# Expert slots of 128 tokens, projection stores from two queues, third parts on VectorE, and a later reciprocal, in a 16-layer kernel

## What is computed

```python
score = einsum('bhqd,bhkd->bhqk', q, k) / sqrt(HEAD_DIM)
attn = softmax(where(causal, score, -inf), axis=-1)
return einsum('bhqk,bhkd->bhqd', attn, v).transpose(0, 2, 1, 3).reshape(B, S, DIM) @ wo + bo
```

```python
expert_ids = argmax(softmax(einsum('btd,ed->bte', x, router_w)), axis=-1)
h = square(relu(einsum('btd,edh->ebth', x, expert_fc)))      # 128 -> 512 channels
out_e = einsum('ebth,edh->ebtd', h, expert_proj)             # 512 -> 128 channels
output = einsum('ebtd,bte->btd', out_e, one_hot(expert_ids))
```

## Time and profile before

| what | value |
|---|---|
| median of three runs | 6275.22 us |
| the profiled execution's own time | 6273.15 us |
| span of that execution on the engines | 6271.4 us |
| mean granted TensorE clock | 0.912 of full |
| TensorE busy | 4874.7 us (78%) |
| VectorE / ScalarE / POOL busy | 3773.5 / 3169.5 / 1644.0 us |

### The profile page before, as it was taken

How to read it: one execution, slowest core, us unless ns; L and a number is a source line. 1 busy time by engine, 2 the same in 40 slices (tenths; PEclk the granted TensorE clock), 3 DMA queues, 4 the chain that set the end, 5 groups by cost and what they waited for, 6 DMA issues and landing times. The chain is left out here.

```text
span 6271.4 us, 90519 instructions
## 1 busy us (share of the span) xinstructions
PE 4874.7 (78%) x33371; PEld 2083.9 (33%) x33466; DVE 3773.5 (60%) x4700; ACT 3169.5 (51%) x5938; POOL 1644.0 (26%) x1264
## 2 busy tenths in 40 slices
PE   5777658886678866688765887849976799688799
PEld 2232223332222235222253222326532244222244
DVE  6899546764677732778424876277738710578510
ACT  5665336665456732367512776534456521477621
POOL 0666137672211124311153111000005500311100
PEclk8999869998889988899986999969988999799999
DMA  0000031110312123321133111000000000101100
GB/s 25 0 1 0 4 101 31 38 36 18 95 34 46 36 62 98 107 45 40 41 99 119 34 41 42 8 10 2 2 13 0 19 0 1 59 23 40 40 0 14
DMA packets 150368, 222.90 MB, mean 36 GB/s; under 512 B 44966, under 2 KB 74514, under 8 KB 148564
## 3 DMA queue, kind: packets, MB, share of 16 engines
q1 hardware_dynamic: 144084, 209.16, 12.2%
q0 software_dynamic: 5888, 8.43, 0.4%
HBM read 137.92 MB, written 81.23 MB: 35 GB/s over the span
## 5 line engine op out<-in xcount | busy, mean ns | idle before, releaser
L914 ACT ACTIVATE l_core_probs<-l_core_ps_scores_b 128x512 f32<-128x512 f32 (+3 forms) x3840 | 1612.7, 500 | 983.7 <-PE l_core_ps_scores_b L826 780.1
L985 DVE TENSOR_REDUCE l_core_chunk_max<-l_core_ps_scores_a 128x2 f32<-128x1024 f32 (+3 forms) x1280 | 1272.1, 1022 | 344.4 <-PE l_core_ps_scores_a L807 180.2
L826 PE MATMUL l_core_ps_scores_b<-l_q_rows_sb,l_k_rows_sb 64*128 64x512 bf16 (+3 forms) x3840 | 943.5, 338 | 265.0 <-ACT l_core_probs L914 222.4
L807 PE MATMUL l_core_ps_scores_a<-l_k_rows_sb,l_q_rows_sb 64*128 64x512 bf16 (+3 forms) x3840 | 763.0, 346 | 252.4 <-DVE l_core_chunk_max L985 148.2
L942 POOL TENSOR_SCALAR_AFFINE_SELECT l_core_probs<-l_core_probs 128x512 f32<-128x512 f32 x512 | 327.3, 639 | 1804.8 <-ACT l_core_probs L914 1804.8
L826 PEld LDWEIGHTS l_core_ps_scores_b<-l_q_rows_sb,l_k_rows_sb 64*128 64x128 bf16 x3840 | 274.4, 94 | 1167.0 <-ACT l_core_probs L914 955.3
L845 PE MATMUL l_core_ps_acc<-l_core_probs,l_v 128*9 128x512 f32 (+3 forms) x6144 | 659.5, 502 | 0.0
L985 DVE TENSOR_REDUCE l_core_neg_max<-l_core_ps_scores_a 128x2 f32<-128x256 f32 (+3 forms) x640 | 504.5, 821 | 82.6 <-PE l_core_ps_scores_a L768 80.8
L1858 POOL TENSOR_TENSOR l_scan_bx<-l_xs,l_scan_b_rows 128x1024 f32<-128x1024 f32 x192 | 452.5, 2357 | 224.1 <-DVE l_scan_states L1868 217.8
L1868 DVE TENSOR_TENSOR_SCAN l_scan_states<-l_scan_ps_decay,l_scan_bx 128x1024 f32<-128x1024 f32 x192 | 439.8, 2290 | 40.7 <-POOL l_scan_bx L1858 15.3
L933 POOL TENSOR_TENSOR l_core_probs_decayed<-l_core_probs,l_decay 128x1536 f32<-128x1536 f32 (+2 forms) x160 | 392.0, 2476 | 218.0 <-ACT l_core_probs L914 217.9
(11 more groups left out here) (316 smaller groups left out, 7391.2 us busy)
## 6 DMA issues: line engine op xcount, KB each, us to landing
l_q_rows<-l_proj_parts SPq DMA_DIRECT2D x96, 256.0 KB, 5.7
l_k_rows<-l_proj_parts SPq DMA_DIRECT2D x96, 256.0 KB, 5.1
l_q_rows_sb<-l_q_rows SPq DMA_DIRECT2D x128, 192.0 KB
l_k_rows_sb<-l_k_rows SPq DMA_DIRECT2D x128, 192.0 KB
l_slots_weights<-m_both_dram SPq DMA_DIRECT2D x46, 512.0 KB
l_heads_out<-l_core_out_sums SPq DMA_DIRECT2D x300, 32.0 KB
l_q_rows_sb<-l_core_max_parts SPq DMA_DIRECT2D x480, 4.0 KB, 1.8
l_core_heads<-l_heads_out SPq DMA_DIRECT2D x15, 512.0 KB, 5.5
```

What stands on the lines that cost most here:

```text
L807: mm = nc.tensor.matmul(slot[:, i, 0:w], qs[n % 3][rows, p, qt * P:(qt + 1) * P], ks[n % 3][rows, p, c * NT:c * NT + w], start=True, stop= ...
L826: mm = nc.tensor.matmul(pb[(m + i) % 3][:, 0:w], ks[n % 3][rows, p, kt * P:(kt + 1) * P], qs[n % 3][rows, p, q0:q0 + w], start=True, stop= ...
L914: nc.scalar.activation(pt[:, ts % RP, j, 0:w], pb[m % 3][:, 0:w], ACT.Exp, scale=scale).then_inc(b_free, 1)
L985: nc.vector.tensor_reduce(to, pa[e % 2][:, :, 0:width_a(qt, c)], AX.X, ALU.max, negate=True).then_inc(a_free, 1)
```

## The change

It makes five edits.

1. Slots have 128 tokens instead of 256, so there are 39 instead of 23. Per slot there is one gather, one scatter, one transpose, four up products of 128 columns and four down products of 128 columns. Buffers: 8 for gathered rows, 8 for weights, 4 for result rows, two PSUM banks for the transpose and four for up. POOL runs gather(j), scatter(j - 6); TensorE's round j is transpose(j + 1), up(j), down(j - 2). The tables of `experts_route` follow.
2. Projection without rope (layers 2, 8, 14): the low part is made by VectorE, which does value(n) and then third(n - 3). Value n waits for the low part of n - 4. POOL keeps the remainder only. The loops over n are unrolled.
3. All projections: the six k stores of each sequence are issued by ScalarE's queue instead of SP's, after the second step of the next sequence, and for the last one at the end.
4. `max_rows` issues three DMAs, each for two partitions 64 apart, instead of six.
5. `invert(B - 1, 12)` moves from ahead of the first late unit to after the addition of late unit 3, ahead of scale_heads(5).

With rope POOL and VectorE do what they did.

```diff
@@ attn_project, sync
-                    for j, n in enumerate("qk"):
-                        for slot in range(6):
-                            sp.dma_start(parts[n]..., part[0:R, j, PAIRS[slot][j], b * S:(b + 1) * S]
+                    for slot in range(6):
+                        sp.dma_start(parts["q"]..., part[0:R, 0, PAIRS[slot][0], b * S:(b + 1) * S]
@@ attn_project, vector (no rope)
+                def plain_value(n):
+                    dve.wait_ge(mm_ready, n + 1)
+                    if n >= 4:
+                        dve.wait_ge(low, n - 3)
...
+                    dve.wait_ge(val, n + 1)
+                    dve.sem_inc(mm_free, 1)
+                def plain_third(n):
+                    dve.wait_ge(mid, n + 1)
+                    nc.vector.tensor_tensor(part[0:R, j, 2, tok], t1[0:R, j, h, :], part[0:R, j, 1, tok],
+                                            ALU.subtract).then_inc(low, 1)
+                    for n in range(4 * B):
+                        plain_value(n)
+                        if n >= 3:
+                            plain_third(n - 3)
+                    for n in range(4 * B - 3, 4 * B):
+                        plain_third(n)
@@ attn_project, scalar
+                def store_k(b):
+                    act.wait_ge(low, 4 * b + 4)
+                    for slot in range(6):
+                        act.dma_start(parts["k"]..., part[0:R, 1, PAIRS[slot][1], b * S:(b + 1) * S]
+                for b in range(B):
                     for m in range(4):
                         first(b, m)
                         if m:
                             second(b, m - 1)
+                        if b and m == 1:
+                            store_k(b - 1)
                     second(b, 3)
+                store_k(B - 1)
@@ attn_project, gpsimd: third, the wait for low and t_free only with rope
@@ attn_core
-        MIN = 16 * 6
+        MIN = 16 * 3
-                    for i in range(2):
-                        for e in range(3):
-                            row = 64 * i + r0 + e
-                            sp.dma_start(qs[u][row:row + 1, :, :].rearrange("o p (k q) -> o (p k) q", q=P),
-                                         mpart[16 * i:16 * i + 16, e, :]).then_inc(m_in, 16)
+                    for e in range(3):
+                        sp.dma_start(qs[u][r0 + e:r0 + e + 65:64, :, :].rearrange("i p (k q) -> i (p k) q", q=P),
+                                     mpart[:, e, :]).then_inc(m_in, 16)
@@ attn_core, vector, late
+                    if t == 3:
+                        invert(B - 1, 12)
                     if t + 2 < TILES:
                         scale_heads(t + 2)
...
                         scale_heads(1)
-                        invert(B - 1, 12)
@@ experts_slots
-SLOT = 2 * P
+SLOT = P
-    XR, YR, WR = 4, 3, 3
-    AHEAD = 3
+    XR, YR, WR = 8, 4, 8
+    AHEAD = 6
-        px = ps("turned_x", [P, NT])
-        pu = ps("up", [P, 2, HC, SLOT])
+        px = [ps(f"turned_x{n}", [P, NT]) for n in range(2)]
+        pu = ps("up", [P, 4, HC, SLOT])
...
-                    if j >= 2:
-                        pe.wait_ge(relu_done, j - 1)
+                    if j >= 4:
+                        pe.wait_ge(relu_done, j - 3)
                     for k in range(HC):
-                        mm = nc.tensor.matmul(pu[:, j % 2, k, :], ...
+                        mm = nc.tensor.matmul(pu[:, j % 4, k, :], ...
...
-                for j in range(SLOTS + 1):
+                for j in range(SLOTS + 2):
                     if j + 1 < SLOTS:
                         turn_in(j + 1)
                     if j < SLOTS:
                         up(j)
-                    if j >= 1:
-                        down(j - 1)
+                    if j >= 2:
+                        down(j - 2)
```

More of the change, by code:

```diff
@@ L501, in _ @@
                     sp.wait_ge(low, 4 * (b + 1))
[L502 to L506 removed]
+                    for slot in range(6):
+                        sp.dma_start(parts["q"].rearrange("(b h s d) t -> b s h d t", b=B, s=6, d=dq)[b, slot],
+                                     part[0:R, 0, PAIRS[slot][0], b * S:(b + 1) * S]
+                                     ).then_inc(stored if b else first_stored, 16)
                     if b == 0:
@@ L584, in second @@
                                          ACT.Copy).then_inc(mid, 1)
-                with act.Fori(0, B) as b:
+                def store_k(b):
+                    act.wait_ge(low, 4 * b + 4)
+                    for slot in range(6):
+                        act.dma_start(parts["k"].rearrange("(b h s d) t -> b s h d t", b=B, s=6, d=dq)[b, slot],
+                                      part[0:R, 1, PAIRS[slot][1], b * S:(b + 1) * S]
+                                      ).then_inc(stored if b else first_stored, 16)
+                for b in range(B):
                     for m in range(4):
@@ L614, in _ @@
                         remain(b, m)
-                        if m:
+                        if m and rope:
                             third(b, m - 1)
@@ L618, in _ @@
                             pool.sem_inc(t_free, 1)
-                    third(b, 3)
-                    pool.wait_ge(low, 4 * b + 4)
-                    pool.sem_inc(t_free, 1)
+                    if rope:
+                        third(b, 3)
+                        pool.wait_ge(low, 4 * b + 4)
+                        pool.sem_inc(t_free, 1)
 def attn_core(net, tag, w, dq, r0, scale, alibi, decay, out_bias, v, qs, ks, heads_out, sums, rsums, consts, c_in,
@@ L1067, in experts_route @@
         count = sb("count", [P, E, 1])
-        above = sb("above", [P, E, NTOK // 2])
+        above = sb("above", [P, E, NTOK])
         need = sb("slots_needed", [P, E + 1])
@@ L1309, in turn_in @@
                 def turn_in(j):
-                    pe.wait_ge(gathered[j % XR], 32 * (j // XR + 1))
-                    if j:
-                        pe.wait_ge(xt_ready, j)
-                    for i in range(2):
-                        mm = nc.tensor.transpose(px[:, i * P:(i + 1) * P], xg[:, j % XR, i, :], net.ident[:, :])
-                    mm.then_inc(px_ready, 1)
+                    pe.wait_ge(gathered[j % XR], 16 * (j // XR + 1))
+                    if j >= 2:
+                        pe.wait_ge(xt_ready, j - 1)
+                    nc.tensor.transpose(px[j % 2][:, 0:P], xg[:, j % XR, :], net.ident[:, :]).then_inc(px_ready, 1)
                 def up(j):
@@ L1330, in down @@
                         pe.wait_ge(yr_ready, j - 1)
-                    for i in range(2):
-                        for k in range(HC):
-                            mm = nc.tensor.matmul(py[j % 2][:, i * P:(i + 1) * P], h[:, j % 2, k, i * P:(i + 1) * P],
-                                                  wt[:, j % WR, (HC + k) * P:(HC + k + 1) * P],
-                                                  start=(k == 0), stop=(k == HC - 1))
+                    for k in range(HC):
+                        mm = nc.tensor.matmul(py[j % 2][:, 0:P], h[:, j % 2, k, :], wt[:, j % WR, (HC + k) * P:(HC + k + 1) * P],
+                                              start=(k == 0), stop=(k == HC - 1))
                     mm.then_inc(py_ready, 1)
                 turn_in(0)
-                for j in range(SLOTS + 1):
+                for j in range(SLOTS + 2):
                     if j + 1 < SLOTS:
@@ L1366, in y_rows @@
                     if j >= YR:
-                        act.wait_ge(scattered[j % YR], 32 * (j // YR))
-                    nc.scalar.copy(yr[:, j % YR, :, :], py[j % 2][:, 0:SLOT].rearrange("p (i c) -> p i c", i=2)).then_inc(yr_ready, 1)
-                for j in range(SLOTS + 1):
+                        act.wait_ge(scattered[j % YR], 16 * (j // YR))
+                    nc.scalar.copy(yr[:, j % YR, :], py[j % 2][:, 0:P]).then_inc(yr_ready, 1)
+                for j in range(SLOTS + 2):
                     if j < SLOTS:
                         relu(j)
-                    if j >= 1:
-                        y_rows(j - 1)
+                    if j >= 2:
+                        y_rows(j - 2)
             @block.vector
```

108 lines of the change are left out of this document (53 added, 55 removed).

## The result

The changed kernel took 6134.93 us in the median of four runs (6124.79 to 6136.52); the kernel before, on the same chip, 6276.62 (four runs, 6273.28 to 6287.34). The ratio is 0.9768, with a 95% interval from 0.9751 to 0.9785. The profiled execution took 6124.79 us, 148.4 less than that of before.

What follows compares the result with a forecast made beforehand. In the expert slots no engine was full: POOL waited for results and TensorE for gathers. From 6273.15 us, slots -105, reciprocal -31, maxima -19 and projection -9 gave 6109, stated as 6110; range 6080 to 6185.

Steps and rivals of the forecast that it cites:

- Slots, -105: Both expert stages: 111.7 us from first gather to last scatter instead of 164.0 and 164.7; -105 us for both.
- I take its waits in the middle at nothing: Expert slots: POOL, six slots ahead, waits nothing mid-stretch as long as other engines need under 2.71 us per slot.
- Rival E: Expert slots: gathers starve behind weight loads; at a landing of 12.5 us, +94 for the slots, 6308 in all; 3%.
- The reciprocal, -31: Last group of the attention cores: moving the reciprocal saves 6.2 us per layer, five layers; -31 us.
- The maxima, -19: Attention cores: three issues instead of six save 1.9 us at the first and last groups, five layers; -19 us.
- I leave it as it was: Landing of the maxima's DMAs, 1.8 us in the median and 3.2 at most, taken as unchanged.
- Projection, -9: Projections: -2 each in layers 2 and 8, 0 in layers 4 and 6, -5 in layer 14; -9 us.
- Four buffers of t1 take up most of that: Projections: buffers mostly absorb VectorE's and POOL's waits of up to 3.8 us behind ScalarE's six issues, three times per layer.
- +10 (every stall on the path): Upper end for all five projection layers together: +10 us, if every stall lies on the path.
- B: Expert slots: VectorE's squares obstruct POOL's DMAs, 3.4 us per slot; -57 instead of -105, 6158 us; 20%.
- C: Attention cores: the reciprocal's wait only moves, to the return of the inverse; 6141 us; 12%.
- D: Expert slots: TensorE stays at 1.2 GHz, 4.3 us per slot; +8 instead of -105, 6223 us; 4%.

Runs made afterwards that it cites:

- the first and the third group: Follow-up runs, each group of four kernels on one chip; the changed kernel without edit took 6166.23 us in the first and 6159.96 in the third.
- the run on record: The changed kernel's original profiled execution, against the kernel before: 6124.79 us.
- the second group: Four follow-up kernels on one chip: changed with six maxima DMAs 6156.87 us, slots' part alone 6170.91, changed with old ring and lead 6575.24, 256-token slots 6211.54.

## Why the prediction was right, and where not

The forecast was 6110 us, the result 6134.93; on the profiled executions -163 against -148.4.

**Slots, -105.** Right in size and in its steps: 112.7 and 109.9 us where 111.7 had been worked out, the first scatter 14.6 and 13.7 us after the first gather (13.5), a slot every 2.75 and 2.71 us on average while gathers and scatters alternate (2.71), most of them 2.65. By itself the part gave -102.5. On the chips of the first and the third group it gave less: the slots stages are 70 and 75 us shorter than in the profile of the kernel before, by late signals that nothing in the forecast stood for. The 6166 and 6160 us there lie in the range by its width, and not because their cause was foreseen. What the forecast took for granted was the lead: "I take its waits in the middle at nothing" holds at six and would have been wrong by 200 us per layer at three, which I had not worked out. Rival E has the chain spread over three slots; by the kernel's order it is four at a lead of six (gather j + 3 is issued right after scatter j - 4). Two small sums are off as well: the end at 1.30 us is -113, not -114, and E's slots come to +93, not +94.

**The reciprocal, -31.** Measured 35.7 over the cores and 33.4 on the clock. What was named as late next came as named: VectorE waits 3.31 us for the inverse (some 4 were forecast) and nobody behind it waits.

**The maxima, -19.** Measured 17.9 over the cores, 17.4 from the timelines before and after. "I leave it as it was", of the landing, held: 1.21 us after the end of the issues against 1.20. What was off is the 1.9 us at the first group, taken from layer 4 alone. In the other four layers the kernel before waits only 1.0 us there, so only that wait and some 0.2 us around it could be gained: the first groups gave 6.9 us in all where 9.5 had been taken, the last ones 10.5 where 9.5 had. That the sum came as near -19 as it did is in part luck. The Trainium skill (DMA: Bandwidth & Descriptors, "Why a DMA increments its semaphore by 16 and not by 1") has the merged DMA on two engines instead of sixteen, with the issuing sequencer writing the rest of the sixteen in one step. The trace agrees: the semaphore has 3 records for each merged DMA (144 for 48 in each layer) and 16 for each of one partition. The longer landing that the prediction took from this, and with it -16, is not there.

**Projection, -9.** Here the sign failed: +14.5. Layer 14 (-3.7, forecast -5; the sign named for it, at least 4 us, is just missed), layers 2 (-1.2) and 8 (+1.5) are within 4 us of the forecast. Layers 4 and 6 came out at +8.0 and +9.8. The step that failed is "Four buffers of t1 take up most of that", with its "0 in layers 4 and 6". Two things were wrong in it. The price of six issues was taken from SP alone, 0.63 us each, 3.8 in all; with SP's stores under way as well it was 7.22 and 6.74 us, and 3.79 only once. And with rotary positions VectorE, POOL and ScalarE pass each buffer round in a ring with no slack: of 7.2 us POOL waited 5.4 and TensorE 4.6. The upper end, "+10 (every stall on the path)", was 4.5 us too low for the same reason.

**The rivals.** B, POOL obstructed by VectorE, has not come, though the forecast's 0.4 us was seen. In the changed kernel's two stretches 49 indirect DMAs that overlapped a square alone took 1.03 us in the mean and 43 that overlapped a square and the copy 1.12, against 1.02 for the 36 that met nothing; in the kernel before, 42 that met a square took 1.19. That is some 5 us over both layers; 19 of the 92 that met a square took over 1.1 us, before 20 of 42. The Trainium skill (SBUF — State Buffer, "Who interferes with whom") says of a VectorE instruction like the square, a tensor_tensor with both inputs in SBUF, that it contends with POOL's reads, and infers that it leaves the writing of descriptors alone. The trace agrees for most: a whole square is 0.69 us, and 73 of the 92 DMAs that met one took no more than 1.1 us; why the other 19 took longer, 16 of them beside a copy too, stays open. C and D (the granted clock is 0.93) did not come either. Nor did E: TensorE waits for gathers 22 times in 39 slots, 29.4 us of 112 in all and 9.7 of them in the first 16 us, but POOL, which sets the pace, hardly waits for its rows.

## What to carry to other kernels

Issuing a DMA costs the issuing engine's own time, and more of it while many stores are under way, so a compute engine that stands in a tight ring of buffers is the wrong place for it; where nothing waits behind it, it is free but brings little as long as the DMA engines are full. The Trainium skill (DMA: Bandwidth & Descriptors, "Issuing engines are not separate DMA queues") says that a second issuing engine saves sequencer time alone; in layers 4 and 6 it hardly saved that: the twelve stores of layer 4's first sequence were issued within 8.9 us by two queues, and within 8.8 by SP alone.

When a loop over slots gets smaller slots, follow its chain through the order of instructions of each engine: the chain's time over the pace wanted (here 7.1 to 8.8 us over 2.65, that is 2.7 to 3.3) is the number of slots that must be under way, and the order adds its own (two here). At a lead of three the same code was 407 us slower than at six.

## What the runs showed of the hardware that was not expected

**Signals of TensorE that come late, on some chips.** On the chips of the first and the third group the slots' stretches took 126 to 131 us, in the run on record and on the chip of the second group 110 to 116, with the same code of the slots. The trace of the changed kernel in the first group shows how (timeline, first expert layer):

```profile
2316.93 1.06 PE L1349 MATMUL l_slots_ps_up<-l_slots_slot_x,l_slots_weights 128*128 128x128 f32 x8
...
2319.78 1.07 PE L1349 MATMUL l_slots_ps_up<-l_slots_slot_x,l_slots_weights 128*128 128x128 f32 x8
...
2323.01 0.60 ACT L1386 ACTIVATE l_slots_relu<-l_slots_ps_up 128x512 f32<-128x512 f32 x1 [4.08 <-remote]
2323.50 0.26 ACT L1392 COPY l_slots_y_rows<-l_slots_ps_down 128x128 f32<-128x128 f32 x1
...
2323.65 0.61 ACT L1386 ACTIVATE l_slots_relu<-l_slots_ps_up 128x512 f32<-128x512 f32 x1
```

ScalarE's relu at 2323.01 reads products whose records end at 2317.99, and all of its other inputs were there; the next one, whose products end at 2320.85, starts right behind it. Over the two stages of that run ScalarE started more than 0.5 us after its last recorded input 40 times, 77 us in all and 4.5 at most; in the run on record and in the two of the second group with this ring never. There are 20 in each of the two layers, so they are no accident of a moment. In the third group the changed kernel had 34 such starts, 65 us; with four weight buffers 10 remained, 10 us, and the stage was no faster. With a lead of three, on the same chip, there was none. So the chip alone does not bring them on. The Trainium skill (NOTIFIC — the notification-queue block, "7.1 Overflow: three behaviours, one of which stalls the engine") describes a path on which recording can hold up an engine; no run here shows that it is this one. What holds the signals stays open.

**An issue takes longer while many stores are under way, and a second queue adds to that.** In layer 14, where the stores are half as large, SP alone took 3.74 to 3.82 us for six, always. In the changed kernel the last sequence's six took 6.26 us from ScalarE and 7.35 from SP, most of them 1.2 to 1.3 us each, in turn: the two queues together issue one every 0.6 us, as SP does alone. In layers 2 to 8 six took SP 3.75 to 5.47 us with all of K on it. That two queues overlap is not enough to make an issue long, though. In layer 4 of the changed kernel ScalarE's second six overlap SP's, and each costs its 0.6 us (timeline):

```profile
1689.79 3.79 ACTq L611 DMA_DIRECT2D l_k_rows<-l_proj_parts  x6
...
1691.41 3.77 SPq L503 DMA_DIRECT2D l_q_rows<-l_proj_parts  x6
```

And of ScalarE's first six, the last two took 1.50 and 1.37 us although SP had begun and ended its last issue before them. What the two queues share is not shown.

**A DMA for two partitions lands no later than two for one:** 1.21 against 1.20 us after the end of the issues in the first group of layer 2, with the issues themselves 2.0 us shorter.
